# Moving small matmuls off TensorE and reordering the last layers of a fused Perceiver-style block

## The reference, cut to what matters

```python
def cross(h, ctx, w_sim, b_sim, W_qv, b_qv):          # h = layernorm(x)
    w1, w2, w3 = w_sim[:256], w_sim[256:512], w_sim[512:]
    Sim = (h @ w1)[:, None] + (ctx @ w2)[None, :] + (h * w3) @ ctx.T + b_sim[0]
    hq_hat = softmax(Sim, axis=1) @ ctx
    Batt = softmax(Sim.max(axis=1))
    hc_bar = Batt @ h
    return concat([h, hq_hat, h * hq_hat, h * hc_bar], -1) @ W_qv + b_qv

def attn(h, Wq, bq, Wk, bk, Wv, bv, Wo, bo):          # 16 heads of 16, no softmax
    q, k, v = rope(h @ Wq + bq), rope(h @ Wk + bk), h @ Wv + bv
    ctx = per_head((q @ k.T / 4) @ v)
    return ctx @ Wo + bo

def ffn(h, W_r, W_k, W_v, mu_r, mu_k):                # prev = rows shifted down by one
    r = sigmoid((mu_r * h + (1 - mu_r) * prev) @ W_r)
    k = (mu_k * h + (1 - mu_k) * prev) @ W_k
    return r * (relu(k) ** 2 @ W_v)

x = x + cross(layernorm(x), ctx, ...)
x = x + attn(layernorm(x), ...)
x = x + ffn(layernorm(x), ...)
```

## Time and profile before

| | |
|---|---|
| median of 3 runs | 112.22 us (112.09 to 112.31) |
| the profiled execution | 112.1 us, of which its span is 110.3 us |
| PE busy | 105.1 us, 95% |
| DVE busy | 93.1 us, 84% |
| ACT busy | 82.4 us, 75% |
| POOL busy | 29.3 us, 27% |
| TensorE clock granted | at full speed in all 40 slices |
| data from HBM | 29.57 MB |

### The profile page before, as it was taken

One profiled execution on the slowest core, in us unless ns is written; L12 is line 12 of the kernel. 1 busy time (PEld: TensorE's weight loads), 2 busy tenths in 40 slices (PEclk: granted clock), 3 DMA queues, 4 the chain that ended last, 5 costly groups with the idle time before them and its releaser, 6 DMA issues.

```text
span 110.3 us, 1855 instructions
## 1 busy us (share of the span) xinstructions
PE 105.1 (95%) x582; PEld 86.4 (78%) x583; DVE 93.1 (84%) x152; ACT 82.4 (75%) x171; POOL 29.3 (27%) x47
## 2 busy tenths in 40 slices
PE   5999999999999999999999999999999998998890
PEld 2368768588858888899899999989898997887680
DVE  1478999999998998999999999999999847674352
ACT  5067668899979989999999899988976725903450
POOL 2239200444043314233242424286330000200100
PEclk9999999999999999999999999999999999999999
DMA  2999999999999999999999999960000000000001
GB/s 72 367 406 423 416 422 422 416 422 422 409 420 417 418 415 423 417 420 442 442 389 423 415 422 425 406 260 0 3 0 0 0 6 0 0 0 0 6 3 48
DMA packets 8220, 29.82 MB, mean 270 GB/s; under 512 B 1042, under 2 KB 1298, under 8 KB 8082
## 3 DMA queue, kind: packets, MB, share of 16 engines
q1 hardware_dynamic: 8064, 29.69, 66.3%
q10 hardware_dynamic: 146, 0.01, 0.1%
HBM read 29.57 MB, written 0.13 MB: 269 GB/s over the span
## 4 chain that ended last, share of the span: by engine, by line
PE 94%; DVE 1%; issue 1%; ACT 1%; DVEq 0%; ACTq 0%
PE mixed_ps L997 18%; PE scores_ps L968 10%; PE mixed_ps L999 9%; PE scores_ps L940 8%; PE scores_ps L944 8%; PE scores_ps L954 8%; PE scores_ps L925 7%; PE scores_ps L910 4%; PE scores_ps L979 3%; PE scores_ps L1090 2%; PE mixed_ps L1142 2%; PE side_ps L1016 1%; PE scores_ps L1155 1%; PE side_ps L1133 1%; PE scores_ps L1016 1%; PE scores_ps L1125 1%
## 5 line engine op out<-in xcount | busy, mean ns | idle before, releaser
L698 DVE TENSOR_TENSOR pair<-raw,pair 128x1024 fp32r<-128x1024 f32 (+2 forms) x42 | 49.0, 1183 | 1.3 <-ACT pair L488 1.0
L488 ACT ACTIVATE pair<-raw 128x512 fp32r<-128x512 f32 (+1 forms) x42 | 34.5, 820 | 3.8 <-DMA raw<-keys_dram 3.4
L997 PE MATMUL mixed_ps<-pair,turned_high 128*128 128x512 f32 x84 | 32.3, 418 | 0.0
L999 PE MATMUL mixed_ps<-pair,turned_low 128*128 128x256 f32 x84 | 23.6, 281 | 0.0
L463 POOL CAST pair<-raw 128x512 fp32r<-128x512 f32 x22 | 13.6, 619 | 27.3 <-DVE pair L698 23.1
L997 PEld LDWEIGHTS mixed_ps<-pair,turned_high 128*128 128x128 f32 x84 | 15.8, 188 | 2.8
L520 ACT ACTIVATE turned_high<-scores_ps 128x512 fp32r<-128x512 f32 (+1 forms) x23 | 13.4, 584 | 4.0 <-PE scores_ps L968 4.0
L721 DVE TENSOR_SCALAR_CACHE_REDUCE neg_scores<-scores_ps,neg_max 128x1024 f32<-128x1024 f32 (+1 forms) x13 | 15.8, 1216 | 0.2
L999 PEld LDWEIGHTS mixed_ps<-pair,turned_low 128*128 128x128 f32 x84 | 16.0, 190 | 0.0
L728 DVE TENSOR_TENSOR turned_low<-scores_ps,turned_high 128x512 fp32r<-128x512 f32 (+1 forms) x23 | 15.3, 667 | 0.2 <-ACT turned_high L520 0.2
L968 PE MATMUL scores_ps<-ident,neg_scores 128*128 128x128 f32 x98 | 14.6, 272 | 0.0
(11 more groups left out here) (189 smaller groups left out, 130.6 us busy)
## 6 DMA issues: line engine op xcount, KB each, us to landing
raw<-keys_dram SPq DMA_DIRECT2D x24, 512.0 KB, 10.0
raw<-rows_dram SPq DMA_DIRECT2D x24, 512.0 KB, 9.2
w<-weights_dram SPq DMA_DIRECT2D x1, 1792.0 KB, 9.9
w<-weights_dram SPq DMA_DIRECT2D x2, 512.0 KB, 10.4
const<-const_dram SPq DMA_DIRECT2D x1, 832.0 KB, 11.5
raw<-keys_last_dram SPq DMA_DIRECT2D x1, 256.0 KB, 10.2
raw<-rows_last_dram SPq DMA_DIRECT2D x1, 256.0 KB, 6.8
x_sb<-x_dram SPq DMA_DIRECT2D x1, 128.0 KB, 2.2
```

The source lines that it names most:

```text
L488: nc.scalar.activation(pair[:, use % PAIR_BUFS, 0, 0:columns], raw[:, slot(item), 0:columns], ACT.Copy)\
L698: nc.vector.tensor_tensor(out=pair[:, use % PAIR_BUFS, 1, 0:columns], in0=raw[:, slot(item), 0:columns], in1=pair[:, use % PAIR_BUFS, 0, 0 ...
L997: nc.tensor.matmul(mixed_ps[:, :].rearrange("p (h d) -> p h d", h=2), probs_high, both[:, :, t * D:(t + 1) * D], start=(k == EARLY and t = ...
L999: last = nc.tensor.matmul(mixed_ps[:, 0:D], probs_low, rows_tile(high, t), start=False, stop=(k == LATE - 1 and end))
```

## The change

- The term `h @ w1 + b_sim` is no longer made on TensorE (six records of L1045 and L1047 go). The host lays `w1` and the bias out in 128 equal rows of 257 numbers (`w1_rows`); SP loads them behind keys 14. VectorE multiplies and sums (`hw1_parts`, `hw1_sum`) just ahead of `keys_low(19)`. The wait for `sim_max` on TensorE moves down by some instructions.
- The centred input is no longer added by TensorE in the tail. ScalarE centres it at the start, TensorE transposes it there (in place of one of nine idle products), ScalarE copies it out behind `keys_high(3)`, and VectorE adds it with the bias when it evicts `x1`. Both halves of `x1` are now evicted by VectorE, and ScalarE reads them from SBUF for the square and `x1_kept_t`.
- In the tail, the transposes of `hq` stand between the features of `normed_t`; k's cosine part is taken ahead of the wait for the norm and scaled in the sum; q's rotary sum comes before the masking of v'k on VectorE, and q's transposes before the product with Wo on TensorE.
- The second norm: VectorE scales the left half of `x2_c`, ScalarE the right half, and each is transposed by itself (a plain transpose in place of the product with a diagonal). One idle product of two goes. The scaling by `mu_k` is split: ScalarE has the left half, VectorE the right one.
- The last sum: GpSimd adds the left half, VectorE the right one.

```diff
-WARM_START, WARM_NORM_2, WARM_SHIFT = 9, 2, 2
+WARM_START, WARM_NORM_2, WARM_SHIFT = 8, 1, 2
-        x_c = sb("x_c", [P, D])
+        x_c = neg_scores[:, S - 2 * D:S - D]
+        x_c_t = sb("x_c_t", [P, DH, P])
# SP
+                if k == 14:
+                    sp.dma_start(w1_rows[:, :], w1_rows_in).then_inc(w1_rows_loaded, 16)
# GpSimd
+            pool.wait_ge(x2_done, 1)
+            pool.wait_ge(mixed_out_done, 1)
+            nc.gpsimd.tensor_tensor(out=x3[:, 0:P], in0=mixed_out[:, 0:P], in1=x2[:, 0:P], op=ALU.add).then_inc(x3_done, 1)
# ScalarE
-            act.dma_start(bias[:, :], bias_in).then_inc(bias_loaded, 16)
+            center_x()
             act.wait_ge(q_done, DH)
...
-                if k == 8:
-                    center_x()
+                if k == 3:
+                    for a in range(DH):
+                        act.wait_ge(x_c_turned, a + 1)
+                        nc.scalar.activation(x_c_t[:, a, :], x_c_turn_ps[a], ACT.Copy).then_inc(x_c_t_done, 1)
...
+            act.wait_ge(rstd_done, 3)
+            nc.scalar.activation(x2n[:, P:D], x2_c[:, P:D], ACT.Copy, scale=ln_rstd[:, 2:3]).then_inc(x2n_done[1], 1)
# VectorE
+                    if k + 2 == 19:
+                        dve.wait_ge(w1_rows_loaded, 16)
+                        dve.wait_ge(normed_done, DH)
+                        nc.vector.scalar_tensor_tensor(hw1_parts[:, :], normed[:, :], 1.0, w1_rows[:, 0:D], ALU.mult,
+                                                       ALU.mult, accum_out=hw1_sum[:, :]).then_inc(hw1_done, 1)
                     if k + 2 < CHUNKS and not is_native(k + 2):
                         keys_low(k + 2)
...
-            nc.vector.tensor_scalar(x1_t[:, 1, :], x1_ps[1], b_c[:, 1, 0:1], None, ALU.add)\
-                .then_inc(x1_high_rows_done, 1)
+            for a, done in ((0, x1_low_rows_done), (1, x1_high_rows_done)):
+                dve.wait_ge(x1_projected, a + 1)
+                nc.vector.scalar_tensor_tensor(x1_t[:, a, :], x1_ps[a], b_c[:, a, 0:1], x_c_t[:, a, :],
+                                               ALU.add, ALU.add).then_inc(done, 1)
...
-            nc.vector.tensor_scalar(rstd_diagonal[:, :], ident[:, :], ln_rstd[:, 2:3], None, ALU.mult)\
-                .then_inc(diagonal_done, 1)
+            nc.vector.tensor_scalar(x2n[:, 0:P], x2_c[:, 0:P], ln_rstd[:, 2:3], None, ALU.mult).then_inc(x2n_done[0], 1)
# TensorE
+            pe.wait_ge(x_c_done, 1)
+            for a in range(DH):
+                nc.tensor.transpose(x_c_turn_ps[a], x_c[:, a * P:(a + 1) * P], ident[:, :]).then_inc(x_c_turned, 1)
...
-            for o in range(DH):
-                nc.tensor.matmul(x1_ps[o], x_c[:, o * P:(o + 1) * P], ident[:, :], start=True, stop=False)
...
-            for a in range(DH):
-                nc.tensor.matmul(x2n_ps[a], x2_c[:, a * P:(a + 1) * P], rstd_diagonal[:, :], start=True, stop=True)\
-                    .then_inc(x2n_turned, 1)
+            for a in range(DH):
+                pe.wait_ge(x2n_done[a], 1)
+                nc.tensor.transpose(x2n_ps[a], x2n[:, a * P:(a + 1) * P], ident[:, :]).then_inc(x2n_turned, 1)
```

More of the change, by code:

```diff
@@ L1083, in _ @@
                 pe.wait_ge(hq_t_done, a + 1)
-                features(1, a, hq_t)
+                for o in range(DH):
+                    feature(1, a, hq_t, o)
             for a in range(DH):
                 pe.wait_ge(h_hq_done, a + 1)
-                features(2, a, h_hq_t, stop=(a == DH - 1))
+                for o in range(DH):
+                    last = feature(2, a, h_hq_t, o, stop=(a == DH - 1))
+                    if a == DH - 1:
+                        last.then_inc(x1_projected, 1)
             def project(out_ps, block_row, a):
@@ L1125, in _ @@
                 nc.tensor.matmul(attn_ps[a], vk[:, a, :], wo_c[:, a, :], start=True, stop=True).then_inc(attn_summed, 1)
-            pe.wait_ge(rotated_done, 2)
-            for a in range(DH):
-                nc.tensor.transpose(q_turn_ps[a], rotated[:, 1, a * P:(a + 1) * P], ident[:, :])\
-                    .then_inc(q_rot_turned, 1)
             for a in range(DH):
```

141 lines of the change are left out of this document (70 added, 71 removed).

## The result

The changed kernel takes 114.1 us (median of 4 runs, 113.70 to 114.53) against 112.27 us of the kernel before (4 runs, 112.09 to 113.93): ratio 1.0158, 95% interval 1.0125 to 1.0192. I had forecast 112.0 us, range 111.4 to 112.5 us. It is 1.8 us slower, and the time lies outside the range.

A forecast was written before the change was run, and what follows sets the result against it. TensorE, VectorE and the DMA queue were taken to run almost without slack, VectorE setting the keys' end, then latency the tail. +0.33 + 0 - 0.29 - 0.10 - 0.25 + 0.17 = -0.14 us gave 112.0 us, range 111.4 to 112.5 us.

The forecast's parts named there:

- The similarities' bias: Key stream: the new load delays the keys, costing 0.33 us instead of saving TensorE's 0.65 us; range +0.05 to +1.16 us.
- The aside of +0.95 us: New load: by the Trainium skill's 0.95 us for a lone 64 KB transfer, its term would be about +0.95 instead of +0.33 us.
- one idle product fewer: Second norm: one idle product less ahead of the left half's transpose, counted as 0.07 us of the gain there.
- x1 (-0.29 us): Tail, hq to x1's variance: 0.22 us from earlier transposes, 0.07 us more from evicting on VectorE.
- the second square is 0.05 us later against its inputs: x1's eviction: VectorE's two halves follow one another, starts 0.27 us apart, which delays the second square by 0.05 us.
- k and q (-0.10 us): Tail, k, v and q up to x2's sum: start at 99.89 instead of 99.99 us, gain between 0 and 0.25 us.
- Second norm (-0.25 us): Second norm: earlier start, plain transpose and shorter handover bring VectorE's mix from 104.06 to about 103.80 us; bounds 0.1 and 0.35 us.
- The last sum (+0.17 us): End of the tail: VectorE's half stands still beside GpSimd's, ending near 108.32 instead of 108.15 us; bounds -0.05 and +0.3 us.
- No delay by the DMA: Rival, key stream: the new load slips into a gap, 0.28 us better, 111.7 to 111.8 us; chance 0.15.
- TensorE keeps its time: Rival, key stream: VectorE is ahead, so +0.33 becomes -0.65 us, time about 111.0 us; chance 0.05.
- Dear small rows: Rival, new load: 1 KB packets cost what mean ones do, queue stands up to 1.16 us, at most 112.8 to 112.9; chance 0.08.
- The tail gives half: Rival, tail: handovers between engines swallow half its gain, -0.25 us instead of 0.47 us, time 112.2 to 112.4 us; chance 0.17.

The follow-up runs named there:

- e2: The changed kernel with 224 bytes of unused SBUF ahead of x, so that raw begins at a multiple of 256: 112.95 us, ratio 1.0051.
- e4: The changed kernel with the bias's products back on TensorE, without the new load and pass, raw at 48896 again: 112.71 us, ratio 1.0011.
- f2: The kernel before plus only the new load behind key 14, read by nobody, raw at 50176: 112.62 us, ratio 1.0030.
- g2: The kernel before with the products of the similarities' bias left out and nothing in their place: 112.42 us, ratio 1.0016.
- h2: The kernel before plus only a VectorE pass of the same shape and place, result unused, raw at 50176: 112.19 us, ratio 0.9984.
- e1: The kernel before with 32 bytes of unused SBUF ahead of the loads' buffers: 113.0 us, ratio 1.0063.
- g1: The kernel before with raw moved 128 bytes further on, to 49024: 112.96 us, ratio 1.0043.
- f1: The kernel before with raw moved 64 bytes further on, to 48960: 113.19 us, ratio 1.0081.
- e3: The changed kernel again, without an edit, on the chip of batch e: 114.02 us, ratio 1.0105; 113.67 us at full clock.
- g3: The kernel before with one idle product instead of two ahead of the second norm's products: 112.34 us, ratio 0.9992.
- batch e: First of four batches of runs, each on another chip beside runs of the kernel before, which has 112.40 us at full clock here.
- g4: e4 with two idle products, x1's last products half by half, v ahead of k's sum, other tail reordering, last sum on VectorE alone: 111.70 us, ratio 0.9929.
- f4: e4 with two idle products instead of one ahead of the second norm's transposes: 112.06 us, ratio 0.9955.

## Why the prediction was wrong

**The similarities' bias (+0.33 us).** Right in size, and in that the load costs and the pass and TensorE's work don't count: +0.37 us between e2 and e4 and in f2. That the saving of 0.65 us is lost is shown by g2, the pass "0 to 0.1 us" by h2. The path of the delay, through ScalarE's sum to the remainder of chunk 22, stays a reading of the traces: the sum starts at 31.05 to 32.34 us in the profiles with the load and at 30.56 to 32.44 us in those without. The sign that I had named, idle time ahead of TensorE's load for chunk 22, is there in kernels without the change too. The aside of +0.95 us used a figure for 64 KB, and this load has 128.5 KB; it cost 0.37 us.

**What failed first: the sum had no term for where the buffers lie.** I took the queue's rate of 419 GB/s as given and priced only the bytes added to it. The diff shows three new tiles ahead of `raw`, and I read them as storage. Their 2080 bytes put every 4 KB row of the loads 32 bytes past a multiple of 256. So the step that failed is the term for the queue: moving `raw` stood in the sum at nothing. It is worth 0.55 us (e1), 0.66 us (g1) and 0.91 us (f1) at full clock in the kernel before, and 1.15 us between e3 and e2. That ScalarE's sum came 0.63 us late instead of 0.33 us doesn't show it by itself: f2, with its buffers well placed, has 0.61 us there. The packets and the times of e1, e2, f1 and g1 carry this point.

**What failed second: one idle product fewer counted as a gain.** I had 0.07 us for it. It gave 0.00 us (2.90 us with both numbers, before and g3), and in the changed tail the clock fell in 19 of 46 runs with one instead of 2 of 36 with two, at some 1.6 us where a trace shows the fall. I had read "full clock" in the earlier trace rows as a property of the kernel; it is one of an execution. That is the +1.58 us of the profiled run. Of the changed kernel's four runs two had it, 114.53 and 114.32 us, the others took 113.88 and 113.70 us. On the chip of batch e the loss at full clock is 1.27 us (e3 against before): 1.15 us for the address, 0.37 us for the load, less the 0.25 us that the other edits give (e4 against before). Of the first four runs' 1.83 us another 0.31 us are the clock's (median 114.10 us, against 113.79 us of the two at full clock), and 0.25 us stay open, which with so few runs is little.

**x1 (-0.29 us): -0.03 us.** The transposes came 0.22 us earlier, as I had it, and TensorE's last product 0.16 us. Then the step "the second square is 0.05 us later against its inputs" failed: it is 0.13 us later. After, then before:

```profile
90.77 0.61 DVE L822 SCALAR_TENSOR_TENSOR hq<-scores_ps,total_inv,acc 128x128 f32<-128x128 f32 x2 [1.15 <-PE scores_ps L1027]
...
93.90 0.35 DVE L846 SCALAR_TENSOR_TENSOR x_t<-side_ps,b_c,x_c_t 128x128 f32<-128x128 f32 x1 [0.22 <-PE side_ps L1037]
94.17 0.34 DVE L846 SCALAR_TENSOR_TENSOR x_t<-scores_ps,b_c,x_c_t 128x128 f32<-128x128 f32 x1
...
95.55 0.16 DVE L857 TENSOR_SCALAR ln_var<-scores_ps 128x1 f32<-128x1 f32 x1 [0.19 <-PE scores_ps L1117]
```

```profile
93.28 0.35 DVE L831 TENSOR_SCALAR x_t<-scores_ps,b_c 128x128 f32<-128x128 f32 x1 [0.48 <-PE scores_ps L1016]
...
94.68 0.16 DVE L842 TENSOR_SCALAR ln_var<-scores_ps 128x1 f32<-128x1 f32 x1 [0.19 <-PE scores_ps L1100]
```

In both kernels the second half of x1 is what the variance waits for. It starts 3.40 us after hq now (94.17 - 90.77) and 3.41 us before (93.28 - 89.87): now behind the first half on the same engine, where it had stood behind TensorE. The further 0.07 us that I had for the variance didn't come either: from the second square to it is 1.01 us in both kernels. g4 confirms the reading: with the first half early, 0.13 us come back.

**k and q (-0.10 us): 0.** The second half of the change's order ate the first. v stands behind k's sum, which waits for k's sine part on the same engine:

```profile
97.01 0.48 DVE L871 SCALAR_TENSOR_TENSOR neg_scores<-neg_scores,ln_rstd 128x256 f32<-128x256 f32 x1
97.41 0.48 DVE L874 SCALAR_TENSOR_TENSOR neg_scores<-scores_ps,ln_rstd,const 128x256 f32<-128x256 f32 x1
...
100.36 0.82 ACT L666 ACTIVATE neg_scores<-scores_ps 128x257 f32<-128x257 f32 x2 [2.98 <-PE scores_ps L1146]
...
100.90 0.45 PE L1150 MATMUL side_ps<-neg_scores 128*128 128x256 f32 x1
```

The kernel before had v ahead of k's sum:

```profile
96.29 0.48 DVE L862 SCALAR_TENSOR_TENSOR neg_scores<-scores_ps,ln_rstd,const 128x256 f32<-128x256 f32 x1
```

From the variance it is 1.86 us to v instead of 1.61 us, 0.25 us of delay where I had 0.1 us, and 4.81 us to the first copy instead of 4.35 us, 0.46 us where I had 0.33 us; x2's sum starts 5.35 us after it, before 5.31 us. The wait that I saw leave at q came back at ScalarE.

**Second norm (-0.25 us): -0.18 us.** Right in kind; the missing 0.07 us is the idle product's share.

**The last sum (+0.17 us): +0.15 us.** Right in size, and in that VectorE's half is held up beside GpSimd's:

```profile
109.97 0.46 POOL L481 TENSOR_TENSOR neg_scores<-neg_scores 128x128 f32<-128x128 f32 x1 [6.46 <-DVE neg_scores L919]
...
110.13 0.45 DVE L923 TENSOR_TENSOR neg_scores<-neg_scores 128x128 f32<-128x128 f32 x1
```

VectorE's half took 0.45 us beside GpSimd, 0.28 us for the first half without it. It ended 0.15 us after GpSimd's, less than the 0.28 us that two halves strictly in a row would give, so a lock-out for the whole instruction, on which the prediction drew, isn't shown here, though GpSimd's end is only roughly known. g4, with both halves on VectorE, has the 0.89 us of before.

**The rivals.** No delay by the DMA, and TensorE keeps its time: refuted by f2 and g2. Dear small rows: refuted as the cause, they took 47 ns each. The tail gives half: the tail's own edits came to -0.06 us in the profiled stages, the clock's stage left out, while the times of e4 and f4 at full clock lie 0.25 and 0.16 us under before's. I had 0.47 us, so this case came nearest of those named, and both big losses stood in none of them.

**What stays open.** How the transposes and the idle product work together on the clock: the kernel before and the changed one differ in both, and only the product was varied within each. Why the packets are longer at such addresses. And whether the shifts of the buffers differ in cost, 0.55 us in e1 and 0.91 us in f1; by their intervals the three don't.

## What to carry to other kernels

A tile that is added ahead of the buffers of a saturated DMA queue is part of the change: look at the byte at which the buffers begin, keep it at a multiple of 256, and compare the packets' durations, since the rate in the profile moved by 2% only (419 to 409 GB/s). When work is taken off an engine that shows no idle time, leave the work out altogether in one run: if the time stays, something else sets the end there, and moving that work can't pay. An idle product in a tail that goes by latency is judged over a dozen runs by how often the clock falls, not by the time of one profile.
